# Latent attention with an int4 feed-forward layer: the prologue's token groups overlapped

## The reference, cut to what matters

```
c_kv = h @ W_dkv + b_dkv            # 1024 -> 128
c_q  = h @ W_dq + b_dq              # 1024 -> 128
k = c_kv @ W_uk + b_uk              # 16 heads x 48
v = c_kv @ W_uv + b_uv              # 16 heads x 64
q_base = c_q @ W_uq + b_uq          # 16 heads x 48
q_rot = rotary(c_q @ W_qr + b_qr)   # 16 heads x 16
k_rot = rotary(h @ W_kr + b_kr)     # 16 heads x 16
q, k = concat(q_base, q_rot), concat(k, k_rot)
attn = softmax(q k^T / 8); out = (attn v) @ W_o + b_o
x = layernorm(h + out)
w = int4(W_ffn)                     # max |W| / 7, rounded, clipped
y = x @ w + bias + (x @ a) @ b
x = layernorm(x + y)
```

## Time and profile before

| what | value |
|---|---|
| median of 3 runs | 2180.2 us (2178.63 to 2186.67) |
| the profiled execution's own time | 2186.7 us |
| its longest span, core 6 | 2185.1 us |
| spans of the 8 cores | 2166.0 to 2185.1 us |
| ScalarE busy, core 6 | 2015.2 us (92%), of which the 2048 exponentials 1932.7 us, 1025 ns each |
| TensorE busy, core 6 | 1886.2 us (86%) |
| VectorE busy | 603.7 us (28%) |
| first exponential starts, cores 0 to 7 | 160.4, 159.2, 152.8, 156.5, 153.3, 157.6, 160.7, 157.8 us |

### The profile page before, as it was taken

How to read it: one execution, slowest core, us unless ns; L and a number is a source line. 1 busy time by engine, 2 the same in 40 slices (tenths; PEclk the granted TensorE clock), 3 DMA queues, 4 the chain that set the end, 5 groups by cost and what they waited for, 6 DMA issues and landing times.

```text
span 2185.1 us, 60695 instructions; the slowest of 8 cores (2166.0 to 2185.1 us)
## 1 busy us (share of the span) xinstructions
PE 1886.2 (86%) x22258; PEld 706.7 (32%) x22544; DVE 603.7 (28%) x1084; ACT 2015.2 (92%) x2177; POOL 261.5 (12%) x303
## 2 busy tenths in 40 slices
PE   5677777898989899898989899898989899998976
PEld 1222233333333333333333333333333333333323
DVE  2451231123222322223222322223222322222225
ACT  3359999999999999999999999999999999999973
POOL 2100000011101100111101100111111100111021
PEclk9899999999999999999999999999999999999998
DMA  9737220022121211222121311222121311223121
GB/s 147 132 95 159 60 84 9 31 76 76 50 84 52 91 43 38 82 73 76 50 87 50 100 33 40 92 62 76 50 90 47 102 31 40 96 89 108 50 69 39
DMA packets 89417, 155.95 MB, mean 71 GB/s; under 512 B 19888, under 2 KB 60080, under 8 KB 89136
## 3 DMA queue, kind: packets, MB, share of 16 engines
q1 hardware_dynamic: 65680, 107.12, 15.6%
q0 software_dynamic: 23456, 44.93, 9.3%
HBM read 109.88 MB, written 40.89 MB: 69 GB/s over the span
## 4 chain that ended last, share of the span: by engine, by line
ACT 67%; issue 15%; PE 5%; DMA 5%; DVE 3%; SPq 2%; ACTq 2%; POOL 0%; DVEq 0%; another core or an unknown queue 0%; POOLq 0%
ACT Psb L943 67%; SPq L464 2%; ACTq L940 1%; DMA osb<-hT 1%; DMA rbc<-rec 1%; DMA bf_sb<-sinT 1%; PE PS L710 1%; DVE rec L1053 1%; PE PS L864 1%; DMA max_scr<-gmax 1%; PE PS L701 1%; PE PS L810 0%; DVE Qsb L1016 0%; PE PS L827 0%; PE PS L719 0%
## 5 line engine op out<-in xcount | busy, mean ns | idle before, releaser
L943 ACT ACTIVATE Psb<-PS 128x1024 bf16<-128x1024 f32 x2048 | 1932.7, 1025 | 31.5 <-PE PS L810 23.4
L810 PE MATMUL PS<-Qsb,Ksb 64*128 64x512 bf16 x4096 | 802.8, 387 | 173.9 <-ACT Psb L943 164.3
L827 PE MATMUL PS<-Psb,Vsb 128*32 128x512 bf16 x8192 | 632.9, 386 | 0.6 <-ACT Psb L943 0.5
L810 PEld LDWEIGHTS PS<-Qsb,Ksb 64*128 64x128 bf16 x4096 | 213.3, 93 | 702.1 <-issue 695.8
L837 PE MATMUL PS<-Psb,ones_sb 128*32 128x256 bf16 x8192 | 403.0, 273 | 3.1 <-DVE rec L1048 2.2
L837 PEld LDWEIGHTS PS<-Psb,ones_sb 128*32 128x32 bf16 x8192 | 221.0, 97 | 223.2 <-issue 6.6
L1076 DVE TENSOR_TENSOR X<-PS,X 128x512 f32<-128x512 f32 x112 | 77.5, 692 | 645.9 <-PE PS L756 301.1
L827 PEld LDWEIGHTS PS<-Psb,Vsb 128*32 128x32 bf16 x8192 | 127.9, 94 | 236.0 <-issue 235.9
L756 PE MATMUL PS<-wbuf,osb 128*128 128x512 bf16 x343 | 111.8, 383 | 16.6 <-issue 16.5
L785 PE MATMUL PS<-wbuf,osb 128*128 128x512 bf16 x349 | 113.2, 383 | 14.7 <-issue 14.1
L1048 DVE COPY rec<-PS 128x256 f32<-128x256 f32 x64 | 27.0, 423 | 344.7 <-PE PS L837 344.7
(11 more groups left out here) (105 smaller groups left out, 654.3 us busy)
## 6 DMA issues: line engine op xcount, KB each, us to landing
wbuf<-wo_p POOLq DMA_DIRECT2D x32, 512.0 KB, 6.9
rbc<-rec SPq DMA_DIRECT2D x512, 32.0 KB, 1.9
X<-h SPq DMA_DIRECT2D x28, 512.0 KB, 4.4
x_scr<-X SPq DMA_DIRECT2D x28, 512.0 KB, 2.7
X<-x_scr SPq DMA_DIRECT2D x28, 512.0 KB, 3.5
wbuf<-wf_p POOLq DMA_DIRECT2D x28, 512.0 KB, 7.0
out<-X SPq DMA_DIRECT2D x28, 512.0 KB, 2.6
X<-W_ffn SPq DMA_DIRECT2D x16, 512.0 KB, 4.8
```

Source lines behind the costliest of these rows:

```text
L810: m = pe.matmul(PS[:, b0 + 512 * hh:b0 + 512 * (hh + 1)], Ksb[rows, k0:k0 + 128], Qsb[rows, 512 * p:512 * (p + 1)], tile_position=(64 * hh ...
L827: pe.matmul(PS[32 * j:32 * (j + 1), b0:b0 + 512], Vsb[:, v0:v0 + 32], Psb[:, p0 + 512 * (j // 2):p0 + 512 * (j // 2 + 1)], start=first and ...
L943: act.activation(Psb[:, 1024 * (g % 4):1024 * (g % 4 + 1)], PS[:, 1024 * (g % 2):1024 * (g % 2 + 1)], AF.Exp, scale=0.125).then_inc(sem["e ...
```

## The change

- `kv_mm(s-1, k)`, the pair k of keys and values of group s-1, is now issued inside the projections of group s: `c_kv` of group s first (8 matmuls), then for k = 0 to 7 one pair of group s-1 and 3 of the 24 matmuls of the rotated keys and of `c_q`. A ninth round (s = 8) has only the pairs of group 7.
- The 10 query matmuls are issued two to a round, at k = 0 and k = 2 of the rounds 1 to 5, into bank 1, and read `c_q` of group 0 straight from `cq_sb`, into which ScalarE now evacuates it. No store and load of it is left for group 0.
- `kra`, `krc`, the tables, and the semaphores of their stores and loads exist twice, by parity of the group. Tables are loaded two groups ahead. SyncE's fetch of the rotated keys of group s-1 stands after the stores of group s.
- The first scores wait for the keys and rotated keys of group 0 only; every fourth chunk of the first pair waits for those of its own group. Values wait for all evacuations, as does the third exponential (it overwrites the value bias).
- GpSimd issues group 1's load before the weights `Wk_cat`, `W_uv` and the value bias; group 0's first half has a semaphore of its own, so that four matmuls can start on it.

The diff's core:

```diff
             for s in range(NSP):
...
-                sp.wait_ge(sem["st_rk"], 32 * (s + 1))
-                sp.wait_ge(sem["ev_kn"], 8 * (s + 1))
...
+                if s + 2 < NSP:
+                    tables_k(s + 2)
+                if s:
+                    sp.wait_ge(sem["ev_cq"], s + 1)
+                    sp.dma_start(out=cq_scr[:, tau:tau + 512], in_=cqst[s % 2]
+                                 ).then_inc(st_cq[s % 2], 16)
+                    rot_load(s - 1)
...
+            for s in range(NSP + 1):
+                if s < NSP:
+                    ckv_mm(s)
                 for k in range(8):
+                    if s:
+                        kv_mm(s - 1, k)
+                    if (s, k) in q0_at:
+                        pe.wait_ge(sem["ev_cq"], s)
+                        q_step(q0_steps[q0_at.index((s, k))])
+                    if s < NSP:
+                        for n in range(3 * k, 3 * k + 3):
+                            kr_cq_mm(s, n)
...
-                    pe.wait_ge(sem["ev_kn"], 8 * NSP)
-                    pe.wait_ge(sem["ev_v"], 8 * NSP)
-                    pe.wait_ge(sem["ld_krot"], 32 * NSP)
+                    pe.wait_ge(sem["ev_misc"], 10)
+                if g < NKC and kc % 4 == 0:
+
+                    pe.wait_ge(sem["ev_kn"], 8 * (kc // 4 + 1))
+                    pe.wait_ge(ld_krot[kc // 4 % 2], 32 * (kc // 8 + 1))
...
+            def kr_evac(s, blk):
+                if s >= 2:
+                    act.wait_ge(st_rk[s % 2], 32 * (s // 2))
+                act.wait_ge(sem["mm_kr"], 2 * s + blk + 1)
+                act.activation((krc if blk else kra)[s % 2], bank(2 + blk), AF.Identity,
+                               bias=bkr_sb[:, blk:blk + 1]).then_inc(sem["ev_kr"], 1)
```

More of the change, by code:

```diff
@@ L425, in q_step, with rot_load @@
                                      ).then_inc(ld_qr[p], 16)
[L427 to L429 removed]
+            def rot_load(s):
                 tau = 512 * s
[L431 to L441, removed]
[L442 to L444 removed]
+                if s >= 2:
+                    sp.wait_ge(ld_krot[s % 2], 32 * (s // 2))
+                sp.wait_ge(st_rk[s % 2], 32 * (s // 2 + 1))
                 sp.wait_ge(sem["ev_kn"], 8 * (s + 1))
@@ L739, in _ @@
-                if s == 2:
-                    q_step(("qr", 0, 0))
-                    q_step(("qr", 0, 1))
-                    for p in range(NP):
-                        q_step(("qp", 0, p))
+                if 8 * s + k >= 2:
+                    pe.wait_ge(sem["ev_kn"], 8 * s + k - 1)
+                pe.matmul(bank(4 + k % 2), wk_sb[:, 128 * k:128 * (k + 1)], ckv
+                          ).then_inc(sem["mm_kn"], 1)
+                i, half = k // 2, k % 2
+                if 8 * s + k >= 2:
+                    pe.wait_ge(sem["ev_v"], 8 * s + k - 1)
@@ L819, in values @@
                 first, last = g % NKC == 0, g % NKC == NKC - 2
+                if g == 0:
+                    pe.wait_ge(sem["ev_kn"], 8 * NSP)
+                    pe.wait_ge(sem["ev_v"], 8 * NSP)
                 if first and P >= 2:
@@ new lines, in _ @@
+                for k in range(8):
+                    if s:
+                        t0 = S * k + 512 * (s - 1)
+                        act.wait_ge(sem["mm_kn"], 8 * (s - 1) + k + 1)
+                        act.activation(Ksb[:, t0:t0 + 512], bank(4 + k % 2), AF.Identity,
+                                       bias=bkc_sb[:, k:k + 1]).then_inc(sem["ev_kn"], 1)
+                    if s < NSP and k == 2:
+                        kr_evac(s, 0)
+                    if s < NSP and k == 5:
+                        kr_evac(s, 1)
@@ new lines, in _ @@
+            for s in range(NSP + 1):
+                a, n0 = kra[s % 2], 5 * s
+                for k in range(8):
+                    if s:
+                        v_evac(s - 1, k)
+                    if (s, k) in q0_at:
+                        q_step(q0_steps[q0_at.index((s, k))])
+                    if s < NSP and k == 3:
+                        dve.wait_ge(sem["ev_kr"], 2 * s + 1)
+                        if s:
+                            dve.wait_ge(sem["rope_k"], n0)
+                        rot_swap(a, krs, "rope_k")
+                    if s < NSP and k == 4:
+                        dve.wait_ge(ld_tabk[s % 2], 32 * (s // 2 + 1))
+                        rot_mult(a, krs, kcos[s % 2], ksin[s % 2], "rope_k", n0)
+                    if s < NSP and k == 5:
+                        rot_add(a, krs, "rope_k", n0)
+                    if s == 1 and k == 7:
+                        q_step(("rope", 0))
```

242 lines of the change are left out of this document (131 added, 111 removed).

## The result

The changed kernel takes 2159.8 us (median; 2157.3 to 2162.1) against 2180.4 for the kernel before in the same comparison, a ratio of 0.990 with the interval 0.9878 to 0.9923. It is 20.5 us faster; the forecast said 38. The profiled execution took 2159.7 us.

A forecast was written before the change was run, and what follows sets the result against it. ScalarE's exponentials bound the kernel, their stream staying fixed; only its start moves, from 160.7 to 122.4 us on core 6. That 38.3 us off the median of 2180.2 gives 2142 us, range 2133 to 2158.

The forecast's parts named there:

- A stream held by ScalarE's own work that the change doesn't touch.: From first exponential to end: claimed unchanged at 2024.4 us on core 6 and 2022.8 on core 0.
- Rival C: After the first exponential: part of the gain lost, the first pair stalling by 12 us, giving 2154 us; chance 0.05.
- The same 38.3 off the median.: Last step of the sum: the slowest core's 38.3 us gain taken off the median of 2180.2, giving 2142 us.
- Pace of a round: TensorE's prologue rounds: 10.78 us with two query matmuls, 10.35 without, interleaving costing nothing, tightest margin about 0.3 us.
- Round 2's start: Prologue: 52.4 us on core 6, held by `wqr`; 54.0 on core 0, where group 2's landing decides.
- First half of group 0 at nothing: Start of prologue: the earlier start on half of group 0 gains nothing, lying before the waits for loads.
- 6.2 us to the first exponential: End of prologue: group 7's pairs, with ScalarE's `c_q` and eight key-tile evacuations plus hand-over, take 6.2 us, formerly 12.5.
- Loads keep up (0, other end 8.5): hT and table loads in the prologue run just ahead of TensorE, costing 0; at worst group 7 lands 8.5 us late.
- SyncE's queue (0): Stores and fetches of rotated keys in the prologue: landing times stay hidden, priced at 0.
- Rival B: TensorE's clock gives way during 64 us of gapless prologue matmuls: rounds 13 us longer, 2155 us; chance 0.05.
- some 2 more: Round 1 after the wait for `wqr`: about 2 us beyond 8.4 at full pace, because TensorE comes from a wait.
- Rivals D and E: Something that stays holds the start, 2160 us; or the loop through SyncE's stores lengthens rounds, 2189 us; chance 0.03 each.

The follow-up runs named there:

- e12: Changed kernel with VectorE's normalising product at the 16th exponential instead of the 12th, only in the third pair of the second to eighth tiles: 2148.0 us, ratio 0.983.
- e8: Changed kernel with 218 more already-met TensorE waits, spread over places where it idles for loads, restoring the earlier alignment of instruction packets: 2151.9 us, ratio 0.985.
- e5: The kernel before, unchanged, measured again for a second profiled execution: 2182.7 us, ratio 0.999.
- e4: Changed kernel with the ten steps of the first queries in rounds 2 to 6 instead of 1 to 5, their rotation too: 2162.4 us, ratio 0.990.
- e1: Changed kernel with 218 more waits, long met, all at the head of TensorE's program: 2155.0 us, ratio 0.987.
- e7: Changed kernel with a group's keys and values multiplied in one block again, instead of one pair between three projections: 2181.7 us, ratio 0.999.
- e6: Changed kernel whose first scores wait for all keys, values and rotation rows, as in the kernel before: 2167.6 us, ratio 0.992.
- e9: Changed kernel with VectorE's normalising product 4 exponentials later in every pair but a tile's last: 2150.3 us, ratio 0.983.

## Why the prediction was wrong

It was right about the prologue and about what holds it, and it missed the time by 17.8 us, which is 1.8 us above its range of 2133 to 2158. It was wrong that nothing else would change. On core 0, the slowest, the miss adds up: 1.1 us in the first exponential (125.1 for 124.0), 10.3 in the stream, and 6.5 in the last step of the sum: 17.9.

- *"A stream held by ScalarE's own work that the change doesn't touch."* This step failed; the sum put the change of the stream at nothing, and it measured 8.9 us in the mean (2016.7 to 2025.6) and 10.3 on core 0. The stream is ScalarE's own work except in a few places, and those hang on when eight small DMAs of SyncE land. The change moved none of these instructions against each other; it moved the packets of TensorE's instructions against them. Shown from both sides: 38 waits make the old kernel lose it, 218 give it back to the new one, 256 do not, and e12 shows by which wait it acts. Rival C had the right side of the first exponential and nearly the right size (12 us), but named the first pair and the loads of W_ffn and W_o; the first tile lost nothing (0.1 us of excess against 1.9).
- *"The same 38.3 off the median."* The profiled execution lay 6.5 us above the median, and the slowest core of it gained more than the others could. Only cores 0 and 6 were worked out, the two that started last; the mean core gained 31.9. A maximum over eight cores whose starts scatter by 8 us falls by less than the unluckiest core does. With the old phase (e8) the changed kernel takes 2151.9, inside the range: 9.9 above the forecast are this step and the first exponentials' scatter. That split is rough, since e8 was measured in another comparison; by its ratio, 0.985 x 2180.4, the time would be 2147, 5 above the forecast, and the phase would cost 13 us instead of 8. How the 6.5 us divides between start and stream stays open, since only the profiled executions show a first exponential (e5).
- *Pace of a round:* right, 10.79 and 10.36 for 10.78 and 10.35. The 0.3 us of margin in the fullest round held.
- *Round 2's start:* 54.67 for 54.0 on core 0, but released by the end of round 1 behind `wqr`, not by group 2. Group 2 had landed at 52.07. e4 shows why that hardly matters: without the wait for `wqr` TensorE waits for group 2 instead, and the slower matmuls after that wait take back most of the 3.4 us.
- *First half of group 0 at nothing:* right, and more than that. In e1 group 0's first projection was done 19 us later, and the price was 3.5 us.
- *6.2 us to the first exponential:* right, 125.10 - 118.87 = 6.23. The 5.5 us in the same step for the last rotated keys are 5.7 by its rows (159.97 - 154.23); nothing hangs on it.
- *Loads keep up (0, other end 8.5):* right; on no core does TensorE wait for hT from round 2 on. *SyncE's queue (0):* right; no wait of ScalarE for a store.
- *Rival B:* not seen in the profiled execution. The granted clock was 1.00 on all eight cores for 60 to 110 us, the 2.4 GHz level, with 234 matmuls in 50.00 us on core 0. The Trainium skill (TensorE: Matmul & The Clock Gate, Part 1) has a die go to 13/16 once three of its cores run dense matmuls; this stretch shows no such step, with all eight cores multiplying. After the wait for `wqr` the clock was 0.66 in 40 to 50 us, which the step's "some 2 more" covered.
- *Rivals D and E:* excluded by the first exponentials.

The forecast's own conditions caught it: the first exponential was where it said, and the stream passed the 2030 us at which it called itself wrong.

Of the 31.9 us of prologue, taking out the interleaving costs 21.1 (e7) and taking out the waits by group 7.1 (e6). Since e7's rounds are slower than the old ones, these two are not shares of the 31.9 that add up, and the tables two rounds ahead, the spread queries and the loads in another order were not taken out one by one.

## What to carry to other kernels

A stretch that a change does not touch can still change its length, when its stalls depend on coincidences: compare the loss per period of the long loop, not only the moment it starts. Where an engine's queue waits for a chain of small DMAs, put that wait behind the work that others need, not in the middle of it; that made this kernel nearly indifferent to the disturbance (e12), although the same move in all pairs cost the first tile 5 us (e9). And when a maximum over cores is forecast, work out every core, not the slowest two.

## What the runs showed of the hardware

- TensorE's instructions come over the DMA engines: 195 packets of 16 KB for 49,987 and 50,025 instructions, 196 for 50,153, 50,243 and 50,281, about one per 256. While one is in flight, an issue of a small DMA by SyncE took up to 3.5 us, where nine in ten issues took 0.51 to 0.60. Over all fourteen profiled executions 1820 of 1874 slow issues had such a packet beside them, though only 43% of the 4190 issues that met one were slow. Another queue of the kind "instruction", with packets of 8 KB, stood beside 45 more; of the 44,487 issues that met neither, 9 were slow. Why the two disturb each other the runs don't show.
- A wait of TensorE that is already met took 0.106 us each where 218 stood in a row.
